# Constant products in TensorE's waits: the head, the first turn and the last batch's tail of a transformer block kernel

## What is computed

```python
mod = (silu(c) @ wmod).reshape(8, 6, 1, 128)          # sa, ca, ga, sb, cb, gb
h = layernorm(x) * (1 + ca) + sa
x = x + ga * attn(h)      # q, k, v; causal softmax(q k^T / sqrt(8)) v; @ Wo + bo; norm * gamma + beta
h = layernorm(x) * (1 + cb) + sb
logits = h @ router       # softmax, the best 2 of 8 experts keep their probability
x = x + gb * (sum_e coef_e * (silu(h @ gate_e) * (h @ up_e)) @ down_e + shared(h))
```

## Time and profile before

| what | value |
| --- | --- |
| median of 3 runs | 563.61 us (563.37 to 567.88) |
| the profiled execution's own time | 562.72 us |
| its span, first to last instruction | 561.0 us |
| PE busy | 501.3 us (89% of the span) |
| DVE, ACT, POOL busy | 375.2, 291.1, 256.5 us |
| mean granted clock of TensorE | 0.957 of full speed |
| head, until the first `s1` | 0 to 34.07 us |
| first turn | 34.07 to about 84.9 us |
| tail, from `o` of the last group | 520.5 to 561.0 us |

### The profile page before, as it was taken

One profiled execution on the slowest core, in us unless ns is written; L12 is line 12 of the kernel. 1 busy time (PEld: TensorE's weight loads), 2 busy tenths in 40 slices (PEclk: granted clock), 3 DMA queues, 4 the chain that ended last, 5 costly groups with the idle time before them and its releaser, 6 DMA issues.

```text
span 561.0 us, 10206 instructions
## 1 busy us (share of the span) xinstructions
PE 501.3 (89%) x3628; PEld 273.6 (49%) x3643; DVE 375.2 (67%) x813; ACT 291.1 (52%) x614; POOL 256.5 (46%) x363
## 2 busy tenths in 40 slices
PE   1657989999999999999999999999999998999386
PEld 1433444554655464556555465546455644554144
DVE  6368986688567757775768756775777476861244
ACT  1103555766467546756575646664675546564220
POOL 6135427724664357625672466435752534244100
PEclk9977799999999999999999999999999999997669
DMA  5264412411432113410342144212341031001000
GB/s 124 73 180 103 128 44 82 156 46 43 100 115 85 45 51 93 157 44 17 88 158 52 34 99 133 68 44 58 88 156 43 2 103 24 3 0 39 0 2 19
DMA packets 46931, 40.66 MB, mean 72 GB/s; under 512 B 8088, under 2 KB 42656, under 8 KB 46880
## 3 DMA queue, kind: packets, MB, share of 16 engines
q1 hardware_dynamic: 39232, 36.92, 23.5%
q10 hardware_dynamic: 7648, 3.09, 2.1%
HBM read 24.91 MB, written 14.68 MB: 71 GB/s over the span
## 4 chain that ended last, share of the span: by engine, by line
PE 65%; DVE 16%; ACT 7%; issue 2%; DMA 1%; POOL 1%; DVEq 0%; POOLq 0%
PE s_bank L1018 10%; PE pv_bank L1047 10%; PE s_bank L1033 8%; PE gate_bank L1100 7%; DVE row_max L856 7%; PE up_bank L1111 6%; PE gate_bank L1133 6%; PE s_bank L1020 4%; PE misc L976 3%; PE misc L998 3%; ACT probs L659 3%; DVE stats_x L799 2%; PE up_bank L1071 2%; ACT square L685 2%; PE misc L1081 1%
## 5 line engine op out<-in xcount | busy, mean ns | idle before, releaser
L856 DVE TENSOR_REDUCE row_max<-s_bank 128x1 f32<-128x512 f32 (+3 forms) x352 | 212.2, 636 | 38.9 <-PE s_bank L1020 35.9
L659 ACT ACTIVATE probs<-s_bank 128x512 f32<-128x512 f32 x320 | 181.4, 597 | 65.3 <-PE s_bank L1033 60.7
L1018 PE MATMUL s_bank<-k_stack,q_stack 72*128 72x256 bf16 (+3 forms) x512 | 133.0, 308 | 13.0 <-DVE row_max L856 6.9
L1033 PE MATMUL s_bank<-q_stack,k_stack 75*128 75x128 bf16 (+3 forms) x512 | 116.9, 305 | 8.2 <-ACT probs L659 6.9
L559 POOL TENSOR_SCALAR_AFFINE_SELECT probs<-probs 128x512 f32<-128x512 f32 (+1 forms) x96 | 76.6, 804 | 88.4 <-ACT probs L659 87.8
L1020 PE MATMUL s_bank<-causal,ident_bf 128*128 128x128 bf16 x512 | 98.9, 223 | 0.0
L1047 PE MATMUL pv_bank<-probs,v_aug 128*32 128x512 f32 (+3 forms) x1024 | 91.4, 454 | 0.4 <-POOL probs L559 0.3
L1018 PEld LDWEIGHTS s_bank<-k_stack,q_stack 72*128 72x128 bf16 x512 | 50.6, 99 | 66.9 <-DVE row_max L856 48.6
L1033 PEld LDWEIGHTS s_bank<-q_stack,k_stack 75*128 75x128 bf16 x512 | 41.7, 98 | 55.5 <-ACT probs L659 25.6
L1020 PEld LDWEIGHTS s_bank<-causal,ident_bf 128*128 128x128 bf16 x512 | 51.0, 100 | 15.2 <-issue 6.2
L544 POOL TENSOR_TENSOR hidden<-hidden,coef_sb 128x512 f32<-128x512 f32 x28 | 35.6, 1273 | 22.1 <-ACT coef_sb L704 22.1
(11 more groups left out here) (150 smaller groups left out, 587.3 us busy)
## 6 DMA issues: line engine op xcount, KB each, us to landing
q_stack<-q_scr SPq DMA_DIRECT2D x96, 96.0 KB
k_stack<-k_scr SPq DMA_DIRECT2D x96, 96.0 KB
k_scr<-k_parts SPq DMA_DIRECT2D x14, 256.0 KB, 2.5
q_scr<-q_parts SPq DMA_DIRECT2D x7, 384.0 KB, 2.3
k_scr<-k_parts SPq DMA_DIRECT2D x7, 384.0 KB, 2.4
x_res<-in_L_attn_x SPq DMA_DIRECT2D x8, 256.0 KB, 3.9
out_x<-out_sb SPq DMA_DIRECT2D x8, 256.0 KB, 2.6
x_in<-in_L_attn_x ACTq DMA_DIRECT2D x7, 256.0 KB, 2.6
```

The source lines that it names most:

```text
L659: nc.scalar.activation(dst, src, ACT.Exp, scale=SCALE).then_inc(exp_done, 1)
L856: nc.vector.reduce_max(row_max[s % 2][:, 0, h:h + nh, qt], s1_bank[u % 2][:, 0:nh * w].rearrange("p (h k) -> p h k", h=nh), AX_X).then_inc ...
L1018: nc.tensor.matmul(dst[:, w * i:w * (i + 1)], q_stack[0:KROWS, h, P * qt:P * (qt + 1)], k_stack[0:KROWS, h, 0:w], start=True, stop=False)
L1033: final = nc.tensor.matmul(dst[:, at:at + w], k_stack[0:MROWS, hh, P * j:P * (j + 1)], q_stack[0:MROWS, hh, P * j:T], start=True, stop=True)
```

## The change

A tile `ones_wide` of 128x512 ones in bf16 is added, which POOL fills with one more memset among the first constants. A function `fill` is called ahead of every task on PE. By three tables it issues 0 to 36 products of the constant identity (`ident_bf`, 128x128, as weights) with `ones_wide`: 128 rows, 512 columns, bf16, into a bank that nothing else uses at that place (`s1_bank[1]` in the head, `up_bank` in the first turn, `pv_bank` in the tail). Nobody reads the results. The products carry no semaphore and wait for nothing, but for `const_done` ahead of the first. They stand ahead of the task's own wait.

```diff
+FILL_START = {("cond", 0): 9, ("xt", 0): 12, ("q", 0): 4, ("k", 0): 6, ("v", 0): 5}
+FILL_FIRST = {(name, a): 1 for name, n in (("s1", U1), ("s2", U2)) for a in range(1, n)}
+FILL_TAIL = {("ot", 0): 3, ("y", 0): 3, ("x2t", 0): 36, ("lg", 0): 3}
...
+        ones_wide = sb("ones_wide", [P, 512], BF16)
...
             nc.gpsimd.memset(ident_bf[:, :], 0.0)
+            nc.gpsimd.memset(ones_wide[:, :], 1.0)
...
+            def fill(it, name, a):
+
+                bank = pv_bank if last(it) else s1_bank[1] if first(it) else up_bank
+                table = FILL_START if first(it) else FILL_FIRST if it == 0 else FILL_TAIL if last(it) else {}
+                if first(it) and name == "cond":
+                    pe.wait_ge(const_done, 1)
+                for _ in range(table.get((name, a), 0)):
+                    nc.tensor.matmul(bank[:, :], ident_bf[:, :], ones_wide[:, :], start=True, stop=True)
...
             def run(it, s, name, a):
+                fill(it, name, a)
                 if name == "cond":
                     condition()
```

## The result

Over 20 runs of each, the changed kernel takes 562.63 us in the median (560.27 to 566.49) and the kernel before 566.87 (562.97 to 568.25). The ratio is 0.995, with a 95% interval from 0.993 to 0.997: the means are 563.01 and 565.92, so 2.9 us less. The gain is real and less than 1%.

What follows compares the result with a forecast made beforehand. Bound: PE's low clock in the head, first turn and tail, with DVE close behind in the first turn's first three stages. Head -2.1, first turn +2.0, tail -4.4 sum to -4.5 us: 558.2, or 559.1 for the median; range 555.0 to 563.8.

Steps and rivals of the forecast that it cites:

- The head: Start to first s1: products raise the clock, so q, k and earlier steps shorten; -2.1 us, between -3.2 and +2.5.
- the terms ahead of q: Head: L955 0.9 us and transposes 0.45 us shorter if the clock rises, against 0.4 us charged for delaying cond.
- Rival 4: Head stays at half clock and its products overrun: +2.5 us in place of -2.1, total 563.7 us; chance 0.05.
- The first turn: 67 products in four stages, -0.3, -1.1, +1.3 and +2.1 us: clock gained early, products cost late; sum +2.0 us.
- Rival 1: First turn hides its products, so stages 3 and 4 cost nothing: -7.9 us, median 555.7 us; chance 0.25.
- Stage 1: First turn's first stage: PE falls behind until the clock rises, then catches up; -0.3 us, between -0.7 and +0.4.
- in the batches between nothing is added, so nothing changes: Batches between first turn and tail: gains or costs from the start are carried to the end unchanged, 0 us.
- The tail: Products ahead of ot, y, x2t and lg keep the clock up for later steps; -4.4 us, up to +6.0.
- rival 3: Tail: the 36 products overrun their wait at half clock, +6.0 us, total 569.5 us; chance 0.05.
- The term for the experts, -2.2: Tail: three expert products need 2.7 us instead of 5.3; 2.2 us counted because of DVE's routing steps.
- PE is then dense, so the clock holds: Tail: PE dense from 520 us, so the clock doesn't fall at 523 and y is 0.8 us shorter.
- rival 2: Clock falls in the tail's wait anyway, only y's 0.8 us is gained: -0.9 us, total 562.7 us; chance 0.2.

Runs made afterwards that it cites:

- e1: The changed kernel with only the head's 36 products kept; 563.21 us mean of 12, 1.4 ± 1.0 less than the kernel before.
- e14: e9 with 19 more products in turn 1's first stage; 560.03 us mean of 10, 5.3 ± 1.9 less than the kernel before.
- e4: The changed kernel without the first turn's 67 products; 561.60 us mean of 12, 3.05 ± 1.4 less than the kernel before.
- e9: The changed kernel without first-turn products in stages 3 and 4, plus one ahead of each last-turn s2 unit from the second; 559.39 us mean of 6.
- e17: e9 repeated unaltered; 559.84 us mean, 5.3 ± 1.3 less than the kernel before.
- e12: The changed kernel with two products in place of one per unit in stages 3 and 4 of the first turn; 570.63 us in one run.
- e6: The changed kernel with the first turn's products in stages 1 and 2 only; 559.60 us mean of 10, 5.8 ± 1.5 less than the kernel before.
- e10: e9 with the coefficients' transposes (ct) moved behind three products of the experts; 560.82 us.
- e18: The changed kernel run once more, unaltered; 562.86 us over 12 runs, 2.3 ± 1.5 less than the kernel before.
- e2: The changed kernel with only the first turn's 67 products kept; 567.31 us mean of 12, 2.7 ± 1.7 more than the kernel before.
- e7: The changed kernel without first-turn products, plus one ahead of each of nine s2 units in the last turn; 558.12 us mean of 6.
- e3: The changed kernel with only the tail's 45 products kept; 563.40 us mean of 12, 1.2 ± 1.5 less than the kernel before.

## Why the prediction was right or wrong

**In short.** Two steps failed in mechanism: that nothing changes in the batches between (+1.9 us in the first stage of turn 1), and, in the tail, that the clock holds behind the 36 products and that the experts then gain 2.2 us (1.1 at full clock, nothing in ten of 15 traces). And the base was too low by 3.3 us.

**The base.** The forecast of 559.1 was 4.5 us below 563.61. The measured median, 562.63, is only 1.0 below that number; against 20 runs of the kernel before the time saved is 2.9 us by the means and 4.2 by the medians. That 4.2 is near 4.5 is luck, and that 562.63 lies within the range owes to the range's width: the terms below are off in both directions. The sum went against one execution that had drawn a short first turn (50.8 us, mean of eight 53.1), and the three runs around it had a median 3.3 us below that of 20. The strip was read slightly wrong too: its low digits in the tail are slices 37 to 39 (505 to 547 us), the last one is a 9.

**The head** (-2.1): right in size (-2.4 in three traces, -1.9 in 15, and -1.4 ± 1.0 in e1's runs), and q and k came as worked out, 1.10 and 1.13. The gain lies behind q's start: from there to the first s1 it is 17.9 us before and 15.9 after. q itself starts at 15.1 to 16.5 us in all 15 traces, and at 15.7 to 16.2 in the five without products. So the terms ahead of q brought little or nothing; for L955 the trace of e14 shows it best:

```profile
7.32 1.06 PE L961 MATMUL up_bank<-cond_T,wmod_sb 128*128 128x8 f32 x8 [0.26 <-DVE cond_T L731]
...
10.82 0.60 PE L995 MATMUL misc<-ident,x_n 128*128 128x128 f32 x4
...
13.60 0.45 ACTq L620 DMA_DIRECT2D wd<-in_L_ffn_shared_down  x1
14.18 0.78 ACT L638 ACTIVATE h1T<-misc,mod_cols 128x512 f32<-128x512 f32 x1 [8.47 <-issue]
15.10 1.10 PE L1018 MATMUL misc<-h1T,wq 128*128 128x512 f32 x2 [2.82 <-ACT h1T L638]
16.04 2.38 PE L987 MATMUL s_bank<-ones_wide,ident_bf 128*128 128x512 bf16 x6
18.21 1.83 PE L1018 MATMUL misc<-h1T,wk 128*128 128x512 f32 x2
```

Here the clock did rise during the first nine, as in eight of the 15 traces (not in the three changed ones, where L961 kept its 1.88). The transposes are done at 11.42, but ACT issues the weights' transfers until 14.05 and writes `h1T` only then, so nothing is gained. The prediction named no such floor. In the 20 traces ACT's last issue ends between 13.9 and 15.1, in the kernel before at 15.10, behind its transposes (14.99). In four of the eight (e4, e9, e14, e17) the clock then fell again, as the prediction feared; in three of them the six products and k ran low in whole or in part, in e17 q did, and the first s1 came at 32.2 to 32.9. Rival 4, the head low throughout, falls.

**The first turn** (+2.0): the sum was near (+1.6), and stages 3 and 4 were priced nearly right: +1.7 for 1.3, +1.9 for 2.1. Rival 1, that they hide, falls: both stages are longer than they are at full clock without products, and e12 shows PE as the bound. Stage 1 (-0.3) failed. Its products don't bring the clock up in time to catch up: the stage's mean is 0.66, it is 0.6 longer, and DVE's busy share there falls from 0.83 to 0.77 where the prediction wanted it up. Over the twelve traces with these products it takes 11.4 (e6, e12) to 12.7 us, against 11.2 to 11.4 without, so this cost differs by execution. Stage 2 (15.0 us) holds.

**Behind the first turn**: the step "in the batches between nothing is added, so nothing changes" failed in the first stage of turn 1. It holds behind that stage, where 408 us are the same within 0.1 in the changed kernel. The low stretch there cost +1.9 in the mean of three traces and stands in no term of the sum. That products in the first turn raise its chance is shown (7 of 10 against 0 of 8); why they do isn't.

**The tail** (-4.4): mis-sized, -2.65 in three traces and -2.4 in 15. y's 0.74 and, at full clock, the transposes' and router's 1.28 are the 0.8 and 1.35 of the prediction, and the 36 fit their wait (7.93 us, ended 1.61 early), so rival 3 falls. Two things failed. The term for the experts, -2.2, measured -1.13 even where the clock held (from `lmax` to the end 22.67 before, 21.54 after): I stopped at DVE's routing steps ahead of the first silu and didn't follow them on. Behind them DVE computes `coef` at 544.41, after silu, hidden and rank; POOL's four steps on it end at 546.47; PE waits for them with three expert products queued behind `ct`. None of these steps is itself faster when PE is. That this wait of 1.24 us is where the missing 1.1 went fits in size but isn't shown: e10, which moved `ct`, ran at the low clock there. The rows of POOL in the changed kernel:

```profile
545.07 0.30 POOL L593 TENSOR_SCALAR coef_parts<-coef 128x32 bf16<-128x32 f32 x1 [8.26 <-DVE coef L925]
545.45 0.24 POOL L595 TENSOR_TENSOR coef_rest<-coef,coef_parts 128x32 f32<-128x32 f32 x1
545.86 0.29 POOL L597 TENSOR_SCALAR coef_parts<-coef_rest 128x32 bf16<-128x32 f32 x1 [0.16 <-POOL coef_rest L595]
546.23 0.24 POOL L599 TENSOR_TENSOR coef_parts<-coef_rest,coef_parts 128x32 bf16<-128x32 f32 x1
```

And the step "PE is then dense, so the clock holds" failed behind the 36. In ten of the 15 traces with the tail's products the clock is low again in the router or in the first expert product, which takes 1.9 to 2.1 us there and 1.1 in the other five. In e18:

```profile
534.33 1.50 PE L1097 MATMUL misc<-w_router,h2T 128*128 128x8 f32 x8 [0.22 <-ACT h2T L686]
535.68 2.05 PE L1116 MATMUL gate_bank<-h2T,wg 128*128 128x512 f32 x2
537.52 1.91 PE L1127 MATMUL up_bank<-h2T,wu 128*128 128x512 f32 x2
...
540.94 1.36 PE L1116 MATMUL gate_bank<-h2T,wg 128*128 128x512 f32 x2
```

Then the tail is 38.35 us instead of 36.7, and from `lmax` to the end all ten take 22.2 to 22.8 us, no less than the kernel before (22.3 to 22.8). So rival 2, given 0.2, happened in part in two executions of three: what it said of the clock came true behind the wait instead of in it, and y, the transposes and part of the router kept their gain.

**One product's price**, 0.22 us at full clock: right, 36 in 7.93 us and 0.21 each in e12. The Trainium skill's rate for a sustained stream (TensorE: Matmul & The Clock Gate, Back-to-back issue gap), about 131 ns, was seen in no stretch of these runs, not even with 21 or 36 in a row.

**Still open**: why products in the first turn make the low stretch of turn 1 likelier; why they cost 2.7 us alone (e2) and nothing visible in company; why the clock holds behind the 36 in some executions only; why e9 isn't better than e7.

## What to carry to other kernels

Constant products paid here where PE waits and PE steps follow on the path to the end (q and k in the head, the tail, the last turn's pv). Where PE is already dense at full clock they cost: 0.09 us each for the first per unit, the full 0.21 for each further one. So look at PE's busy share, stage by stage, before adding them. Follow the chain around a sped-up step through every engine, in its own order too (ACT's transfers ahead of `h1T`, POOL's four steps ahead of `ct`), before its gain is counted. And when the clock is what a change is about, take several traces of both kernels: a single pair here gave +1.2 us where 20 runs of each gave -2.9.

## What the runs showed of the hardware

- Identical instructions got their low clock in different places from one execution to the next: the first turn, without products in it, took 50.8 to 57.7 us. In e3 it was in stage 4 (16.08 us instead of 12.36):

```profile
78.00:92.00 14.00, 12.43 (x73) 5.34 (x69) 7.25 (x12) 6.51 (x12) 3.25 (x7) 0.63 0.17 42
```

- The clock fell behind stretches without a long wait. In the changed kernel it is 1.00 until 517 us and low behind it. From 515 to 517 PE is busy for 1.60 of 2.00 us, and its waits since 513.8 are 0.18, 0.20 and 0.20 us:

```profile
515.00:517.00 2.00, 1.60 (x9) 0.45 (x7) 0.55 (x2) 2.00 (x5) 0.24 (x1) 1.00 0.39 117
517.00:524.00 7.00, 6.68 (x41) 1.89 (x40) 0.00 (x0) 3.09 (x6) 3.37 (x4) 0.53 0.00 0
524.00:537.90 13.90, 11.56 (x61) 5.85 (x59) 4.24 (x16) 3.45 (x14) 2.52 (x4) 0.99 0.00 1
```

  In the low stretch itself PE is busy for 6.68 of 7.00 us, since its products take twice as long there; the clock column tells what was granted, and a full busy share in such a row doesn't mean that much work was done. With products ahead of the last s2 units, e7's same pv stayed at the full clock. In the tail of e18 the fall comes behind the wait of 1.6 us for x_n and short steps.
- The granted clock reads 1.00 in the head, before its first change in the records, while the durations there are those of 1.2 GHz (q 2.04 us at "1.00", 1.12 later). In a stretch ahead of the first change the durations tell the clock, the column doesn't.
